# Four attention layers on one core: TensorE, not VectorE and GpSimd, sums the softmax weights of the last layer in the last two batches

## The chip, the cores and the metric

The kernel runs on one core of a Trainium2 chip. The metric is the time of one execution on the device in microseconds (us). Names of engines: PE is TensorE (PEld its weight loads), DVE is VectorE, ACT is ScalarE, POOL is GpSimd, SP is SyncE, which issues the DMAs.

## What is computed

Input x is 8 x 256 x 32 x 32 in fp32: 8 batches, 256 channels, T = 1024 tokens. Four layers follow one another, each per batch. Only the last one is changed:

```python
def _L3_conv_ref(hidden_states, ...):
    x = _group_norm(hidden_states, gn_gamma, gn_beta)
    x = x.reshape(B, C, H * W).transpose(0, 2, 1)
    q, k, v = x @ wq.T + bq, x @ wk.T + bk, x @ wv.T + bv      # 8 heads of 32 channels
    scores = jnp.einsum('bhid,bhjd->bhij', q * scale, k)        # 1024 x 1024 per head
    probs = jax.nn.softmax(scores)
    ctx = jnp.einsum('bhij,bhjd->bhid', probs, v)
    out = _layer_norm(ctx @ wo.T + bo, ln_gamma, ln_beta)
    return out + residual
```

Layers 0 to 2 (a latent attention, an attention with 32 channels of queries, an attention over all 256 channels with a group norm) are untouched. The softmax needs, for each query, the sum over 1024 keys of the weights exp(score - maximum). Who makes that sum in batches 6 and 7 of layer 3 is what changes.

## The kernel before

**Two lanes.** The program is written as five instruction streams, one per engine, with semaphores between them. Layers 0 to 2 of a batch are its front, layer 3 its back. The front of batch b + 2 runs beside the back of batch b; at the end no front is left, and the backs of batches 6 and 7 run beside each other. Batch 6 uses the tiles of lane `ba` (stacked queries `qs` and keys `ks`, values `vb`, weights `prb`, sums `accb`, banks 4 to 7 of PSUM); batch 7 uses lane `bb` (the tile `q2k` for queries and keys, `xm` for values, `pr`, `acc`, `tmp` and `xm` for weights, `w` for sums, banks 0 to 3).

**The order.** Each engine's stream for two batches is merged from two generators by a table of numbers, `ORDER[part, engine]`: so many pieces of the first, so many of the second, and so on. The part "backs" is the end of the program, with batches 6 and 7. A piece ends at a `yield`.

**A round.** The back of a batch does four heads at a time (QUAD = 4) and so has two rounds, u = 0 and 1. In a round PE first makes 32 tiles of plain scores (`max_tile`, L673, two matmuls each) of which DVE takes the maxima (`maximum`, L1358, 128 x 1024 each); the maxima go by DMA into a row of the stacked queries. Then come 16 steps (`steps`): one step is half of the queries (ic) against one of 8 tiles of keys. A step has four shifted scores (`scores` and `stacked_scores`, L687), one per head, each in one PSUM bank of 512 columns; ACT takes the exponential of each (`exps3`, L1211) into one of RING = 3 slots of weights. Every two steps (RUN = 2) PE multiplies weights and values (`weigh`, L974) for both steps: four matmuls of 32 output rows a step, in four column tiles of the array side by side, into bank 2. I call the 8 matmuls of one `weigh` a run, and the four of a step a quad. A round has 8 runs, a batch 16.

**Banks of the scores.** A score goes to `turn3[use % 3]`, that is banks 0, 1, 3 in turn, and waits until the bank's last tenant has been read (`take_turn`).

**The sums before.** DVE adds the weights of steps pair by pair into `sums` (`add_weights`, L1527, 128 x 1024: two heads at once). In batches 6 and 7 (`both_add`) DVE does the first pair of heads only, POOL the second (L607). After 8 steps PE sums the result over partitions with ones (`sum_weights`, L986, a quad) into one of the three banks, ACT makes 1 / sum from it by Ln and Exp (`invert`, L1078 and L1081), and DVE multiplies (`normalise`, L1534). ACT may reuse a slot of the ring only when the run and both adds that read it are done.

**The tail.** After both rounds come the output projection (L654), the layer norm's variance (L1014) and the rest (L1261 to L1279, L1581, L1585), and the store.

What one step costs PE now, in the kernel's words:

```python
for s in range(first, first + RUN):
    jt = s % NT
    for g in range(QUAD):
        mm = pe.matmul(o.ps[L * g:L * g + L, 2, :],
                       o.vb[:, jt, L * (QUAD * u + g):L * (QUAD * u + g + 1)],
                       weights3(o, STEPS3 * u + s, g), start=jt == 0, stop=jt == NT - 1,
                       tile_position=(0, L * g))
```

Of the kernel before, what the change touches and what calls it, by code (L numbers as in the profile page):

```python
# [29 lines left out]
ALU = mybir.AluOpType  # L30
# [7 lines left out]
CH = C // P  # L38
IC, IW = 2, 512
# [20 lines left out]
for _name, _n in (("gn_w2", 2), ("gn_b2", 2), ("bq2", 2), ("bk2", 2), ("bo2", 2), ("gn_w3", 2), ("gn_b3", 2),  # L60
# [48 lines left out]
        8, 74, 74, 51, 1, 2, 8, 1, 1, 2, 1, 2, 1, 1, 3, 1, 1, 1, 1, 1, 1, 1, 2, 1, 4, 3, 4, 1, 1, 1, 1, 2, 3,  # L109
        2, 1, 1, 5, 1, 3, 1, 17, 1, 8, 1, 3, 1, 1, 1, 5, 1, 4, 1, 2,),  # L110
# [16 lines left out]
        0, 2, 1, 12, 14, 10, 1, 1, 1, 1, 1, 1, 1, 1, 10,),  # L127
# [5 lines left out]
        6, 4, 3, 1, 4, 2, 1, 1, 2,),  # L133
# [67 lines left out]
def attention_layers(nc, x, weights, vectors, small, concepts, constants, out):  # L201
    with ExitStack() as ctx:
# [216 lines left out]
        def both_add(b):  # L419

            return b >= B - 2

        def score_use(s, g):
            return QUAD * s + g + (s >= NT + 2)
# [47 lines left out]
        def _(sp):  # L472
# [9 lines left out]
            def program(o):  # L482
# [26 lines left out]
                def back(b):  # L509
# [16 lines left out]
                    for pair in range(2):  # L526
                        sp.wait_ge(o.summed3[pair].sem, o.summed3[pair].at(b, (NT - 1) * IC * CH - 2))
# [18 lines left out]
        def _(pool):  # L546
# [7 lines left out]
            def program(o):  # L554
# [41 lines left out]
                def back(b):  # L596
                    yield "head"
                    for n in range(IC * CH if both_add(b) else 0):
                        for j in range(1, NT):
                            s = NT * n + j  # L600
                            pool.wait_ge(o.exped[3].sem, o.exped[3].at(b, QUAD * (s + 1)))
# [1037 lines left out]
```

## Time and profile before

| | |
|---|---|
| median of 3 runs | 2710.54 us (2708.7 to 2719.36) |
| the profiled execution | 2716.84 us |
| its span, first to last instruction | 2715.0 us |
| granted PE clock, mean | 0.940 of full |
| PE busy | 2536.3 us (93%) |
| DVE busy | 1870.5 us (69%) |
| ACT busy | 1281.9 us (47%) |
| POOL busy | 591.2 us (22%) |

Times of rows count from the start of the span. The stretch in which batches 6 and 7 stand alone goes from 2372 us to the end. "MATMUL x16" in a row of the trace stands for 8 matmuls of the program, since an fp32 matmul is executed as two; matmuls that read rounded operands (L673, L687) are one each. The bracket at a row's end is the idle time before it and who ended it. In the rows of stretches, the number before "(x" is busy time, and PEclk is the granted clock as a share of full speed: 0.50 is 1.2 GHz, 1.00 is 2.4 GHz.

### The profile page before, as it was taken

How to read it: one execution, taken by the hardware profiler on the slowest of the kernel's cores; microseconds unless marked ns; L12 is line 12 of the kernel's file. 1: busy time of each engine (PE TensorE's matmuls, PEld its weight loads, DVE VectorE, ACT ScalarE, POOL GpSimd, SP SyncE). 2: the span in 40 equal slices, each digit the busy share in tenths (PEclk: the TensorE clock that was granted, in tenths of full speed). 3: DMA queues.
4: the chain of work that ended last, by engine and by line, in shares of the span. 5: the costliest groups of instructions: out<-in, count | busy, mean ns of one | idle time of the engine just before them, and what ended most of it. 6: DMA issues, size and time to landing. Idle time of an engine off the chain costs nothing.

```text
span 2715.0 us, 26577 instructions
## 1 busy us (share of the span) xinstructions
PE 2536.3 (93%) x9892; PEld 1431.6 (53%) x9892; DVE 1870.5 (69%) x1925; ACT 1281.9 (47%) x2209; POOL 591.2 (22%) x322
## 2 busy tenths in 40 slices
PE   7989989999999999999999999999999999988887
PEld 4466654464654656455564646546564555544432
DVE  5544327787487865787677874878657876769995
ACT  2453221646346562555526464364625555135466
POOL 0083130050110502023010401105010130124463
PEclk8999996999999899999999999998999999978898
DMA  2000002020302003020120203010030201222201
GB/s 76 1 0 1 1 17 62 1 47 16 93 1 47 1 24 86 1 47 1 62 47 1 47 1 109 1 39 9 16 93 1 47 1 47 47 62 47 47 16 47
DMA packets 33777, 88.93 MB, mean 33 GB/s; under 512 B 10608, under 2 KB 10800, under 8 KB 33392
## 3 DMA queue, kind: packets, MB, share of 16 engines
q1 hardware_dynamic: 33648, 87.23, 12.0%
q8 instruction: 78, 1.28, 0.2%
q14 instruction: 51, 0.42, 0.1%
HBM read 19.79 MB, written 16.78 MB: 13 GB/s over the span
## 4 chain that ended last, share of the span: by engine, by line
PE 75%; DVE 15%; ACT 4%; issue 3%; POOL 2%; SPq 1%; DMA 1%; DVEq 0%; ACTq 0%; POOLq 0%
PE ps L654 11%; PE ps L687 10%; PE ps L673 9%; PE ps L805 8%; PE ps L974 7%; PE ps L896 6%; PE ps L662 6%; PE ps L809 4%; DVE ba_nmx L1358 2%; PE ps L743 2%; PE ps L882 2%; DVE fa_nmx L1358 2%; DVE accb L1527 2%; DVE bb_nmx L1358 1%; DVE w L1527 1%
## 5 line engine op out<-in xcount | busy, mean ns | idle before, releaser
L1358 DVE TENSOR_REDUCE ba_nmx<-ps 128x1 f32<-128x1024 f32 x448 | 531.3, 1219 | 115.9 <-PE ps L673 114.1
L1211 ACT ACTIVATE prb<-ps 128x512 f32<-128x512 f32 x896 | 483.9, 604 | 220.4 <-PE ps L687 215.5
L1527 DVE TENSOR_TENSOR accb<-accb,prb 128x1024 f32<-128x1024 f32 x312 | 396.1, 1303 | 78.0 <-ACT prb L1211 77.1
L687 PE MATMUL ps<-qs,ks 97*128 97x512 f32 x896 | 349.4, 479 | 20.9 <-DMA qs<-ba_nmx_r 16.3
L1069 ACT ACTIVATE pr<-ps 128x512 f32<-128x512 f32 x336 | 198.2, 604 | 334.8 <-PE ps L896 260.4
L673 PE MATMUL ps<-ks,qs 96*128 96x512 f32 x896 | 333.3, 471 | 17.7 <-DVE ba_nmx L1358 15.8
L576 POOL TENSOR_TENSOR q2k<-pr,q2k 128x512 fp32r<-128x512 f32 x112 | 147.7, 1338 | 797.5 <-ACT q2k L1106 797.5
L687 PEld LDWEIGHTS ps<-qs,ks 97*128 97x128 f32 x896 | 170.5, 203 | 215.2 <-issue 101.7
L673 PEld LDWEIGHTS ps<-ks,qs 96*128 96x128 f32 x896 | 175.3, 206 | 122.5 <-DVE ba_nmx L1358 51.4
L974 PE MATMUL ps<-prb,vb 128*32 128x512 f32 x1792 | 230.0, 633 | 0.2 <-ACT prb L1211 0.2
L1358 DVE TENSOR_REDUCE fa_nmx<-ps 128x1 f32<-128x1024 f32 x168 | 198.0, 1216 | 34.1 <-PE ps L882 18.9
L566 POOL TENSOR_TENSOR acc<-pr 128x1024 f32<-128x1024 f32 x28 | 67.4, 2407 | 689.9 <-ACT pr L1069 576.6
L805 PE MATMUL ps<-pr,h 128*128 128x512 f32 x448 | 210.7, 593 | 0.0
L809 PE MATMUL ps<-q2k 128*128 128x512 f32 x672 | 179.8, 404 | 5.3 <-ACT tmp L1097 4.1
L566 POOL TENSOR_TENSOR acc<-acc,pr 128x1024 f32<-128x1024 f32 x56 | 133.6, 2386 | 217.5 <-ACT pr L1069 217.4
L654 PE MATMUL ps<-hb,w 128*128 128x512 f32 x368 | 172.5, 613 | 2.5 <-ACT hb L1127 2.5
L896 PE MATMUL ps<-q2k 128*128 128x512 f32 x672 | 173.4, 393 | 0.0
L809 PEld LDWEIGHTS ps<-q2k 128*128 128x128 f32 x672 | 129.1, 194 | 41.1 <-POOL q2k L576 10.2
L896 PEld LDWEIGHTS ps<-q2k 128*128 128x128 f32 x672 | 126.7, 189 | 37.3 <-issue 10.3
L654 PE MATMUL ps<-h,w 128*128 128x512 f32 x272 | 128.3, 600 | 2.0 <-ACT h L1127 1.5
L805 PEld LDWEIGHTS ps<-pr,h 128*128 128x128 f32 x448 | 84.0, 189 | 64.7 <-issue 56.3
L687 PE MATMUL ps<-q2k,ks 97*128 97x512 f32 x224 | 100.1, 470 | 13.9 <-ACT pr L1069 8.4
(329 smaller groups left out, 3528.7 us busy)
## 6 DMA issues: line engine op xcount, KB each, us to landing
qs<-part SPq DMA_DIRECT2D x168, 128.0 KB, 2.5
ks<-part SPq DMA_DIRECT2D x168, 128.0 KB, 2.5
xm<-in_x SPq DMA_DIRECT2D x8, 1024.0 KB, 4.8
kept<-xm SPq DMA_DIRECT2D x8, 1024.0 KB, 4.2
prb<-kept SPq DMA_DIRECT2D x14, 512.0 KB, 3.7
out<-prb SPq DMA_DIRECT2D x28, 256.0 KB, 2.0
q2k<-part SPq DMA_DIRECT2D x48, 128.0 KB, 2.4
w<-in_weights SPq DMA_DIRECT2D x1, 2592.0 KB, 8.8
```

What stands on the lines that cost most here:

```text
L566: pool.tensor_tensor(o.acc[:], before if jg == 1 else o.acc[:], now, ALU.add).then_inc(o.summed[n].sem, 1)
L654: mm = pe.matmul(o.ps[0:m, bank, :], wcol(name, kt, m0, m), src[:, kt, cols(ic)], start=kt == 0, stop=kt == CH - 1)
L673: mm = pe.matmul(o.ps[:, bank + jc, :], queries[0:STACK, tile(it)], keys[0:STACK, cols(jc)], start=True, stop=True)
L687: return pe.matmul(o.ps[:, bank, :], keys[0:ROW + 1, tile(jt)], queries[0:ROW + 1, cols(ic)], start=True, stop=True)
L805: mm = pe.matmul(o.ps[:, 2 + ch, :], o.v[:, jt, tile(ch)], o.pr[:, t % 4, :], start=jt == 0, stop=jt == NT - 1)
L809: mm = pe.matmul(o.ps[:, 2 + ch, :], values[:, jt, tile(ch)], weights[t % 3], start=jt == 0 and weights is o.p_hi and values is o.v_hi, st ...
L896: mm = pe.matmul(o.ps[:, bank, :], kpart[:, kt, keys], qpart[:, kt, cols(ic)], start=False, stop=kt == CH - 1 and kpart is o.kl2)
L974: mm = pe.matmul(o.ps[L * g:L * g + L, 2, :], o.vb[:, jt, L * (QUAD * u + g):L * (QUAD * u + g + 1)], weights3(o, STEPS3 * u + s, g), star ...
L1069: act.activation(o.pr[:, t % 4, :], o.ps[:, bank, :], ACT.Exp).then_inc(o.exped[n].sem, 1)
L1211: act.activation(weights3(o, n, g), o.ps[:, turn3[score_use(s, g) % 3], :], ACT.Exp)\
L1358: dve.tensor_reduce(o.nmx[:, head, it:it + 1], o.ps[:, bank:bank + 2, :], AX.XY, ALU.max, negate=True).then_inc(o.max_sb[n].sem, 1)
L1527: dve.tensor_tensor(o.sums[pair], o.pairs[(now - 1) % RING][pair] if j == 1 else o.sums[pair], o.pairs[now % RING][pair], ALU.add).then_in ...
```

## The change

In batches 6 and 7 (`pe_sums`) a run of PE gets, behind the four matmuls of a step with the values, four more with ones in the place of the values, in the same column tiles, accumulated over the 8 steps into bank 3 of the lane. The adds of DVE and POOL in these batches are gone, and so are `sum_weights` and the waits on the adds. Bank 3 is no longer free for scores, so these go to banks 0 and 1 in turn, and a score waits for the exponential of the score two before. ACT takes Ln from bank 3 as soon as the run that ends 8 steps is done. The tables of the part "backs" are new for PE, ACT, DVE, POOL and SP (of PE's only the first line is shown).

```diff
     ("backs", "PE"): (
-        2, 1, 6, 1, 1, 1, 6, 1, 2, 5, 1, 2, 1, 7, 1, 4, 1, 5, 1, 3, 1, 6, 1, 2, 1, 2, 1, 6, 1, 1, 1, 8, 1, 3,
...
+        0, 1, 2, 1, 8, 1, 7, 3, 1, 2, 1, 3, 1, 4, 2, 5, 1, 7, 2, 11, 1, 2, 1, 7, 1, 1, 1, 1, 1, 8, 1, 2, 1, 4,
...
     ("backs", "DVE"): (
...
+        27, 4, 16, 1, 7, 1, 1, 6, 1, 1, 4, 22, 1, 5, 31, 1, 4, 3, 1, 2, 1, 2, 4, 2, 4,),
     ("backs", "POOL"): (
-        0, 2, 1, 12, 14, 10, 1, 1, 1, 1, 1, 1, 1, 1, 10,),
+        1,),
...
-        def both_add(b):
+        def pe_sums(b):
             return b >= B - 2

-        def score_use(s, g):
-            return QUAD * s + g + (s >= NT + 2)
+        def score_use(b, s, g):
+            return QUAD * s + g + (s >= NT + 2 and not pe_sums(b))
+
+        def score_bank(b, use):
+            return use % 2 if pe_sums(b) else turn3[use % 3]
...
                         def take_turn(use):
-                            if use >= 3:
+                            if pe_sums(b):
+                                if use >= 2:
+                                    pe.wait_ge(o.exped[3].sem, o.exped[3].at(b, QUAD * STEPS3 * u + use - 1))
+                            elif use >= 3:
                                 done, count = bank_use(o, u, use - 3)
                                 pe.wait_ge(done.sem, done.at(b, count))
-                            return turn3[use % 3]
+                            return score_bank(b, use)
...
                             if first % NT == 0 and n:
                                 pe.wait_ge(o.taken[3].sem, o.taken[3].at(b, n // NT))
+                                if pe_sums(b):
+                                    pe.wait_ge(o.logged[3].sem, o.logged[3].at(b, n // NT))
                             for s in range(first, first + RUN):
...
+                                for g in range(QUAD if pe_sums(b) else 0):
+                                    mm = pe.matmul(o.ps[L * g:L * g + L, 3, :], ones[:, 0:L],
+                                                   weights3(o, STEPS3 * u + s, g), start=jt == 0, stop=jt == NT - 1,
+                                                   tile_position=(0, L * g))
                             mm.then_inc(o.weighed[3].sem, 1)
...
-                            if s == NT + 1:
+                            if s == NT + 1 and not pe_sums(b):
                                 sum_weights(0)
                                 yield
                         weigh(STEPS3 - RUN)
                         yield
-                        sum_weights(1)
-                        yield
+                        if not pe_sums(b):
+                            sum_weights(1)
+                            yield
...
                 def invert(b, n, count, bank, into):
-                    act.wait_ge(o.total[n].sem, o.total[n].at(b, count))
+                    if n == 3 and pe_sums(b):
+                        act.wait_ge(o.weighed[3].sem, o.weighed[3].at(b, NT // RUN * count))
+                    else:
+                        act.wait_ge(o.total[n].sem, o.total[n].at(b, count))
...
-                                chunk, j = divmod(n - RING, NT)
-                                used = (NT - 1) * chunk + max(j, 1)
-                                act.wait_ge(o.summed3[pair].sem, o.summed3[pair].at(b, used))
+                                if not pe_sums(b):
+                                    chunk, j = divmod(n - RING, NT)
+                                    used = (NT - 1) * chunk + max(j, 1)
+                                    act.wait_ge(o.summed3[pair].sem, o.summed3[pair].at(b, used))
...
-                            for pair in range(1 if both_add(b) else 2):
+                            for pair in range(0 if pe_sums(b) else 2):
```

The new lines move the numbers: L673 is L662 in the changed kernel, L687 is L676, L654 is L643, L974 is L968, and the matmuls with ones are L973.

In PE's stream, first place: steps of batch 6 in its first round (`qs,ks` are its scores, `prb` its weights), with the maxima of batch 7's first round (`q2k`) between. Before:

```order
L974 MATMUL ps<-prb,vb 32x512 x8
L687 MATMUL ps<-qs,ks 128x512 x2
L673 MATMUL ps<-q2k 128x512 x2
L687 MATMUL ps<-qs,ks 128x512 x3
L673 MATMUL ps<-q2k 128x512 x2
L687 MATMUL ps<-qs,ks 128x512 x3
L974 MATMUL ps<-prb,vb 32x512 x8
```

The changed kernel, near the same place:

```order
L973 MATMUL ps<-prb,ones 32x512 x4
L676 MATMUL ps<-qs,ks 128x512 x2
L662 MATMUL ps<-q2k 128x512 x4
L676 MATMUL ps<-qs,ks 128x512 x2
L662 MATMUL ps<-q2k 128x512 x2
L676 MATMUL ps<-qs,ks 128x512 x2
L662 MATMUL ps<-q2k 128x512 x2
L968 MATMUL ps<-prb,vb 32x512 x4
L973 MATMUL ps<-prb,ones 32x512 x4
L968 MATMUL ps<-prb,vb 32x512 x4
L973 MATMUL ps<-prb,ones 32x512 x4
```

A run has gone from two quads to four, and between runs there are still 6 to 8 scores and two or more tiles of maxima.

Second place, PE's stream from the last run of batch 6 (`prb`) on, where batch 7 (`q2k`) has only itself beside it and the tail of batch 6. Before:

```order
L974 MATMUL ps<-prb,vb 32x512 x8
L986 MATMUL ps<-accb,ones 32x512 x4
L687 MATMUL ps<-q2k 128x512 x2
L654 MATMUL ps<-hb,w 128x512 x4
L687 MATMUL ps<-q2k 128x512 x3
L654 MATMUL ps<-hb,w 128x512 x4
L974 MATMUL ps<-acc,xm 32x512 x2
L974 MATMUL ps<-tmp,xm 32x512 x2
L974 MATMUL ps<-xm 32x512 x4
L687 MATMUL ps<-q2k 128x512 x3
```

The changed kernel:

```order
L676 MATMUL ps<-q2k 128x512 x4
L643 MATMUL ps<-hb,w 128x512 x4
L676 MATMUL ps<-q2k 128x512 x2
L643 MATMUL ps<-hb,w 128x512 x4
L676 MATMUL ps<-q2k 128x512 x2
L968 MATMUL ps<-acc,xm 32x512 x2
L968 MATMUL ps<-tmp,xm 32x512 x2
L973 MATMUL ps<-acc,ones 32x512 x2
L973 MATMUL ps<-tmp,ones 32x512 x2
L968 MATMUL ps<-xm 32x512 x4
L973 MATMUL ps<-xm,ones 32x512 x4
```

The sum with ones that stood behind batch 6's last run is gone, and eight scores now surround the projections, not five; five runs of batch 7 follow in either kernel.

## Rows read from the trace of the kernel before

**Rows 1.** Stretches between landmarks of the end; columns: busy time by engine, PEclk, DMA.
```profile
2413.70:2479.70 66.00, 59.13 (x255) 27.03 (x255) 58.94 (x40) 35.51 (x68) 36.87 (x14) 0.82 0.12 26
2479.70:2558.90 79.20, 69.54 (x292) 32.02 (x288) 68.38 (x57) 40.70 (x76) 37.44 (x14) 0.87 0.13 29
...
2648.70:2692.50 43.80, 39.27 (x159) 13.90 (x156) 30.08 (x15) 27.98 (x53) 25.28 (x10) 0.89 0.02 7
2692.50:2715.00 22.50, 11.73 (x28) 4.96 (x24) 9.08 (x13) 14.21 (x23) 0.00 (x0) 0.80 0.38 128
```

**Rows 2.** Waits of PE, 2413 to 2692: us in total, times, longest.
```profile
PE ps L673 <- DVE bb_nmx L1358: 11.7, 12, 2.5
PE ps L986 <- issue: 6.8, 1, 6.8
PE ps L673 <- DVE ba_nmx L1358: 6.5, 5, 2.6
PE ps L986 <- DVE w L1527: 3.6, 2, 3.2
```

**Rows 3.** Groups of DVE and POOL, 2413 to 2692: busy, mean ns, idle before.
```profile
L1358 DVE TENSOR_REDUCE bb_nmx<-ps 128x1 f32<-128x1024 f32 x57 | 66.8, 1214 | 6.8 <-PE ps L673 6.8
L1527 DVE TENSOR_TENSOR accb<-accb,prb 128x1024 f32<-128x1024 f32 x24 | 55.3, 2305 | 0.5
...
L607 POOL TENSOR_TENSOR accb<-accb,prb 128x1024 f32<-128x1024 f32 x24 | 66.4, 2768 | 28.5 <-ACT prb L1211 27.8
```

**Rows 4.** The same view of DVE from 200 to 2370, where POOL adds no such weights.
```profile
L1527 DVE TENSOR_TENSOR accb<-accb,prb 128x1024 f32<-128x1024 f32 x288 | 340.7, 1219 | 77.5 <-ACT prb L1211 77.1
```

**Rows 5.** PE in order of time: start us, us; runs, tiles of maxima, scores.
```profile
2448.89 1.92 PE L974 MATMUL ps<-prb,vb 128*32 128x512 f32 x16
...
2452.76 0.63 PE L673 MATMUL ps<-q2k 96*128 96x512 f32 x2
2453.22 1.17 PE L687 MATMUL ps<-qs,ks 97*128 97x512 f32 x3
2454.38 1.92 PE L974 MATMUL ps<-prb,vb 128*32 128x512 f32 x16
...
2616.03 1.92 PE L974 MATMUL ps<-prb,vb 128*32 128x512 f32 x16
2617.88 0.96 PE L687 MATMUL ps<-q2k 97*128 97x512 f32 x3
...
2635.21 1.06 PE L974 MATMUL ps<-xm 128*32 128x512 f32 x8
2636.09 1.04 PE L974 MATMUL ps<-pr,xm 128*32 128x512 f32 x8
```

**Rows 6.** PE and ACT in order of time; layer 0, where scores have two banks.
```profile
84.45 0.73 PE L687 MATMUL ps<-q2k,ks 97*128 97x512 f32 x2
...
84.99 1.08 ACT L1069 ACTIVATE pr<-ps 128x512 f32<-128x512 f32 x2 [3.06 <-PE ps L687]
...
86.12 0.73 PE L687 MATMUL ps<-q2k,ks 97*128 97x512 f32 x2
```

**Rows 7.** Stretches from the first to a last run of three rounds.
```profile
2419.90:2474.80 54.90, 48.27 (x213) 21.88 (x212) 50.07 (x32) 30.43 (x59) 36.70 (x14) 0.84 0.06 13
2497.40:2552.30 54.90, 49.64 (x221) 22.60 (x220) 48.74 (x35) 30.91 (x59) 33.45 (x14) 0.85 0.00 1
2571.60:2609.60 38.00, 33.11 (x149) 15.96 (x148) 37.33 (x31) 18.06 (x34) 18.21 (x8) 0.91 0.08 17
```

**Rows 8.** Two stretches of 4 us in which the granted clock fell.
```profile
2432.00:2436.00 4.00, 3.62 (x13) 1.89 (x17) 4.00 (x4) 1.57 (x3) 2.65 (x2) 0.51 0.00 0
...
2668.00:2672.00 4.00, 3.40 (x14) 1.17 (x17) 4.00 (x3) 3.71 (x8) 3.09 (x2) 0.87 0.01 2
```

**Rows 9.** PE in order of time: batch 6's last sum, batch 7's projections.
```profile
2646.80 1.94 PE L986 MATMUL ps<-accb,ones 128*32 128x512 f32 x8 [6.79 <-issue]
...
2692.49 8.30 PE L654 MATMUL ps<-h,w 128*128 128x512 f32 x16
```

More of the change, by code:

```diff
@@ L108 @@
     ("backs", "ACT"): (
-        8, 74, 74, 51, 1, 2, 8, 1, 1, 2, 1, 2, 1, 1, 3, 1, 1, 1, 1, 1, 1, 1, 2, 1, 4, 3, 4, 1, 1, 1, 1, 2, 3,
-        2, 1, 1, 5, 1, 3, 1, 17, 1, 8, 1, 3, 1, 1, 1, 5, 1, 4, 1, 2,),
+        8, 74, 74, 49, 1, 1, 2, 2, 1, 1, 3, 1, 1, 2, 3, 1, 1, 1, 1, 2, 2, 1, 1, 2, 4, 1, 1, 1, 3, 2, 2, 1, 2,
+        2, 5, 1, 1, 1, 10, 1, 1, 3, 8, 1, 4, 1, 2, 1, 14, 1, 3, 1, 4, 1, 2,),
     ("fronts", "DVE"): (
@@ L132 @@
     ("backs", "SP"): (
-        6, 4, 3, 1, 4, 2, 1, 1, 2,),
+        6, 4, 3, 1, 4, 1, 1, 1, 1, 1, 1,),
 }
@@ L525, in back @@
                     sp.wait_ge(o.weighed[3].sem, o.weighed[3].at(b, CH * STEPS3 // RUN - 1))
-                    for pair in range(2):
+                    for pair in range(0 if pe_sums(b) else 2):
                         sp.wait_ge(o.summed3[pair].sem, o.summed3[pair].at(b, (NT - 1) * IC * CH - 2))
@@ L597, in back @@
                     yield "head"
[L598 to L601, printed above, removed]
-                            if j == 1 and n:
-                                pool.wait_ge(o.total[3].sem, o.total[3].at(b, n))
-                            done = o.summed3[1]
-                            if j > 1:
-                                pool.wait_ge(done.sem, done.at(b, (NT - 1) * n + j - 1))
-                            pool.tensor_tensor(o.sums[1], o.pairs[(s - 1) % RING][1] if j == 1 else o.sums[1],
-                                               o.pairs[s % RING][1], ALU.add).then_inc(done.sem, 1)
-                            yield
                 return front, back
@@ L960, in scores @@
                             for g in (2 * pair, 2 * pair + 1):
-                                bank = take_turn(score_use(s, g))
+                                bank = take_turn(score_use(b, s, g))
                                 stacked_scores(bank, o.queries[:, g, :], o.keys[:, g, :], jt, ic).then_inc(o.scored[3].sem, 1)
@@ L1204, in exps3 @@
                                 act.wait_ge(o.weighed[3].sem, o.weighed[3].at(b, (n - RING) // RUN + 1))
-                                chunk, j = divmod(n - RING, NT)
-                                used = (NT - 1) * chunk + max(j, 1)
-                                act.wait_ge(o.summed3[pair].sem, o.summed3[pair].at(b, used))
+                                if not pe_sums(b):
+                                    chunk, j = divmod(n - RING, NT)
+                                    used = (NT - 1) * chunk + max(j, 1)
+                                    act.wait_ge(o.summed3[pair].sem, o.summed3[pair].at(b, used))
                             if n == g == 0 and o.before(b) is not None:
                                 act.wait_ge(o.stored.sem, o.stored.at(o.before(b), 16 * 4))
-                            act.activation(weights3(o, n, g), o.ps[:, turn3[score_use(s, g) % 3], :], ACT.Exp)\
+                            act.activation(weights3(o, n, g), o.ps[:, score_bank(b, score_use(b, s, g)), :], ACT.Exp)\
                                 .then_inc(o.exped[3].sem, 1)
@@ L1241, in steps @@
                         for s in range(STEPS3):
-                            if s == NT + 2:
-                                yield from invert(b, 3, IC * u + 1, turn3[total_use(0) % 3], o.rdenb[:])
+                            if s == (NT + 1 if pe_sums(b) else NT + 2):
+                                yield from invert(b, 3, IC * u + 1, 3 if pe_sums(b) else turn3[total_use(0) % 3], o.rdenb[:])
                             yield from exps3(u, s, 0)
@@ L1250, in steps @@
                         yield
-                        yield from invert(b, 3, IC * u + 2, turn3[total_use(1) % 3], o.rdenb[:])
+                        yield from invert(b, 3, IC * u + 2, 3 if pe_sums(b) else turn3[total_use(1) % 3], o.rdenb[:])
                     def nothing(u):
@@ L1568, in steps @@
                                 yield from normalise(u, 0)
-                            for pair in range(1 if both_add(b) else 2):
+                            for pair in range(0 if pe_sums(b) else 2):
                                 if s % NT:
```

1 line of the change is left out of this document (removed), and 13 rows, old and new, of the table ORDER.

## The prediction, written before the changed kernel ran

> **What bounds the kernel now.** The whole page says PE 93% busy, but the change touches only the end, so I read the stretches between landmarks first, from the first shifted score of batch 6 at 2413.7 us to the end [rows 1]. They take 301 us. Call them B (steps of batch 6 beside maxima of batch 7), C (the reverse), D (second steps of 6 beside second maxima of 7), E (steps of both), F (steps of 7 alone, with the tail of 6) and G (the tail of 7). In B and C the busy columns of PE and DVE are alike, near 90% each, and the granted clock is 0.82 and 0.87: part of PE's busy time is work at 1.2 GHz. PE's waits name the cause [rows 2]: 18.2 us for a DVE maximum, the rest for a sum that DVE or POOL had not finished. DVE is late because its own adds are slow: 2305 ns here [rows 3] against 1219 ns for the same instruction where POOL adds nothing [rows 4]; POOL's own take 2768 ns. Behind such a wait PE's clock falls, as at 2432, where 4 us had 0.51 of the full clock [rows 8]. So the end is bound by DVE with POOL at its side, and PE pays twice, by the wait and by the clock.
>
> **What the change removes.** DVE loses 56 adds of a pair of heads (28 per batch, 7 per sum), 24 of them the accb row at 2305 ns: some 120 us of DVE, and POOL loses its whole part, 56 at about 2.75 us. DVE keeps the maxima, 1214 ns each [rows 3], three per run at most in B and C, so it is idle half the time, and none of PE's waits in rows 2 has a reason any more. PE loses 8 sums with ones, 1 us each.
>
> **What it adds to PE.** A run of two quads occupies PE for 1.85 us (2616.03 to the next start at 2617.88) and a further quad for 0.88 us (2635.21 to 2636.09) [rows 5]. Four quads are 1.85 + 2 x 0.88 = 3.6 us. There are 32 runs, so 56 us more, less 8 us of sums: 48 us of PE at full clock, none of it beside other PE work. Against it stand the waits of PE that the change can end, 11.7 + 6.8 + 6.5 + 3.6, 29 us [rows 2], and the work done at half clock: by the clocks of B, C and F, 0.82, 0.87 and 0.89 [rows 1], it averaged about 0.86, that is 28% of 279 us at 1.2 GHz, some 78 us, which at 2.4 GHz would have been 39. 29 + 39 - 48 = 20 us of gain, if PE could always be fed. I don't think that it can.
>
> **The two banks.** With two banks, a score can be issued only when the exponential two before has ended. Where layer 0 works with two banks [rows 6], the exponentials start 0.54 us after the scores (84.45 to 84.99), two of them take 1.08, so the second starts 0.48 after the first and one lasts 0.60, and the next scores follow 0.05 later (86.07 to 86.12). A pair of exponentials thus costs at least 0.60 + 0.05 + 0.54 = 1.19 us without anything between. During a run PE has at most two scores lying ready, so ACT does two exponentials and then idles; the other six of the two steps must follow in 3 pairs. From one run's start to the next: run 3.6, first score to exponential 0.54, two full pairs 2 x 1.19, the last pair 0.48 + 0.60, and 0.3 for the last score before the run: 7.9 us. A tile of maxima is 0.46 us to the next start, at 2452.76 [rows 5], and some 0.1 more where scores wait; such tiles partly fit the 0.7 us that PE has free in each pair, so I take 8.1 in B and C with about two tiles a run, and 8.8 in D, where the order has about six.
>
> Now the stretches of runs before [rows 7]. B: seven intervals in 54.9 us, 7.84 each; after 7 x 8.1 = 56.7, **+1.8**. C: the same 54.9, **+1.8**. D: four intervals in 38.0 us, 9.5 each; after 35.2, **-2.8**. Before and after these intervals the longer last run (+1.75) and the sums and waits gone (about -1.1 and -0.7) cancel: 0.
>
> E, counted from D's last run (its start is about 2609.6) to the first score behind batch 6's last sum (2648.7): 39.1 us before, of which 6.8 are the wait for POOL's sum and 1.9 the sum at half clock [rows 9]. After: seven runs, four of batch 6 from 2609.6 on and three of batch 7, so 7 x 3.6 = 25.2, and 49 scores in five groups; four banks over two batches let ACT run at 0.48 an exponential, of which four are hidden by each run. I come to 17 us for the groups, 42 in all: **+3**.
>
> F: 43.8 us before [rows 1]. After: 9 us for eight scores round two blocks of projections (four matmuls each, some 3.5 us, a little under half of the 8.30 for eight [rows 9]), five runs at 3.6 = 18, then stretches of 5.0 and 5.2 (with the variance of batch 6, two matmuls of about 0.9 in the gaps) and two of 4.3: 45.8, **+2**.
>
> G: 22.5 us [rows 1], starting with the projections of 8.30 us, in part at half clock [rows 9]. Ln now follows the last run at once, but half of the projections (4 us) hides Ln, Exp and the multiplication anyway, so only the clock can give: **-0.7**.
>
> Sum at full clock: 1.8 + 1.8 - 2.8 + 3 + 2 - 0.7 = +5. Then the clock. At 2668 it fell to 0.87 although PE showed 3.40 us of work in 4 [rows 8], in exactly F's pattern of single scores behind exponentials with gaps of 0.2 to 0.4 us. In the changed kernel this pattern is the rule. I charge one fall more in F than before: a run at half clock is 3.6 us longer; with it **+8 us**. The Trainium skill, page "TensorE: Matmul & The Clock Gate", section "A second HAM failure mode: psum-queue depth-cycling", says that cycling through PSUM banks with micro-idles between groups makes the clock oscillate; by that rule every run of B, C and F would be at risk, not one.
>
> Another rule would raise the price of a quad. "TensorE: Matmul & The Clock Gate", "Measured speedup vs the span model", gives three column tiles of 512 columns a speedup of 2.38, not 3. By it an estimate for a quad would be some 25% above a perfect one, about 0.2 us more, and 56 quads more would add 11 us to the sum; the row of 0.88 us is of this kernel's own quads, about one fourth of four projection matmuls, and decides.
>
> Against the profiled execution's 2716.84 us the sum is 2725; that execution lies 6.3 us above the median of the runs, so I forecast 2719 us, 0.3% above 2710.54. A measurement of this kernel tells about 0.5% (13.6 us) from no change.
>
> **The bounds.** The period of 7.9 us holds only if PE stands in the chain as I say. If maxima fill the gaps completely and scores are never late, the least is PE's own work: a run, eight scores at 0.23 (three take 0.96 us [rows 5], two 0.73 [rows 6]), two tiles and 0.3 for the switches: 3.6 + 1.9 + 1.1 + 0.3 = 6.9 us; then B and C give 8 us more each, D 3, E 5: -24 against my sum, 2695. The other bound is a period of 8.6 with a fall of clock at every third run: below, 2750.
>
> **Rivals.** (1) *PE fed after all, faster* (chance 0.23). Place: B and C, where the best interval of runs was 5.5 us with three banks (2448.89 to 2454.38 [rows 5]). For it: DVE and POOL were what PE waited for [rows 2], and the clock below 0.87 [rows 1] came from these waits; with the adds gone it returns. Against it: two banks do not allow a period under 7.9. It decides from a mean period in B and C of 7.2 us on. Time: 2719 - 24 = 2695. (2) *The clock* (chance 0.34, slower). Between runs PE has 8 scores of 0.23 us and two tiles of 0.46, 2.8 us of work in 4.4 us; in F 1.9. If every third of the 21 intervals of B, C and F falls, the run behind it takes 7.2, not 3.6 us, and the scores about 0.5 us more: 7 x 4.1 = 29 us, less the one fall that I have: 2719 + 25 = 2744. It decides from four falls on. For it: rows 8; against it: the first of these rows stands behind a wait of over 2 us, and the change takes such waits away. (3) *The adds were hidden and the sums' waits are all* (0.05): E and G give back 6.8 + 3.2 us, and the rest stays as before, 2703; PE's waits for DVE [rows 2] speak against it. My own case, the two effects nearly in balance, has 0.38.
>
> **Numbers.** My case spans 2706 to 2730. The range reaches to the middle of (1) and past that of (2): 2694 to 2750, leaving out 2 in 10. Faster by over 0.5% is under 2697: most of (1), nothing else: 0.23. Slower is over 2724: nearly all of (2) and the upper end of my case: 0.37. The rest, 0.40, is within.
>
> **What would show it.** The adds gone from DVE and POOL; starts of runs (L968, first of `vb`) 3.6 us before the next score, and 7.9 to 8.3 apart in B and C at full clock; ACT idle 2 to 3 us in each period, ended by PE's scores; PE's longest waits short and for ACT, none over 1 us for DVE before E's end; clock over 0.95 in B to E. I am wrong if the periods are under 7.2 us, if the clock in B to F is no better than the 0.86 of before, or if a run of four quads takes clearly more than 3.6 us at full clock.

## The result and the profile after

Before 2711.86 us (median of 4 runs), after 2752.24 us (2749.29 to 2753.53): the change makes the kernel 1.43% slower, ratio 1.0143, 95% interval 1.0121 to 1.0166. I had forecast 2719 us and a range to 2750; the result lies 2 us beyond it. The profiled execution took 2753.53 us, its span is 2751.7 us, 36.7 more than before.

The stretches of the end of the changed kernel, in the order B, C, D, E, F, G (columns as in [rows 1]):

```profile
2416.30:2494.20 77.90, 72.96 (x366) 29.76 (x366) 26.04 (x23) 37.73 (x69) 0.00 (x0) 0.87 0.06 13
2494.20:2582.70 88.50, 81.10 (x401) 34.59 (x400) 44.40 (x44) 40.41 (x73) 0.00 (x0) 0.92 0.15 35
2582.70:2641.00 58.30, 53.58 (x274) 25.41 (x270) 38.97 (x36) 28.73 (x52) 0.00 (x0) 0.94 0.19 42
2641.00:2682.90 41.90, 39.38 (x236) 13.91 (x236) 0.00 (x0) 22.82 (x45) 0.00 (x0) 0.92 0.07 26
2682.90:2730.40 47.50, 43.34 (x227) 15.82 (x223) 4.09 (x6) 31.16 (x57) 0.00 (x0) 1.00 0.10 33
2730.40:2751.70 21.30, 10.55 (x28) 4.46 (x24) 9.08 (x13) 13.87 (x22) 0.00 (x0) 0.85 0.19 74
```

Against [rows 1], B is 11.9 us longer and C 9.3. D and E together are 10.4 longer, F 3.7, G 1.2 shorter, and B begins 2.6 us later. The DVE column fell as forecast (59 to 26 us in B) and POOL's is 0. PE's columns rose, and the clock of B and C is 0.87 and 0.92: it came back only in part, and of B to E none reaches the 0.95 that I had named as a sign. In F it is 1.00.

PE's waits from 2413 to 2692, the same view and stretch as [rows 2]:

```profile
PE ps L676 <- ACT prb L1214: 5.3, 16, 0.7
PE ps L662 <- DVE bb_nmx L1361: 3.0, 6, 1.4
PE ps L676 <- DVE part L1356: 2.4, 1, 2.4
```

The waits for a sum are gone, and those for DVE's maxima fell from 18 us to 4. One of these is still 1.4 us, and one for another result of DVE 2.4, where I had expected none over 1 us. New are the many short waits for an exponential: 34 with those of batch 7's tiles, 10.7 us in all, none over 0.7. One interval of runs in B, in PE's order of time (start, duration; the bracket is the idle time before the row):

```profile
2442.64 0.99 PE L676 MATMUL ps<-qs,ks 97*128 97x512 f32 x2 [0.41 <-ACT prb L1214]
2443.83 0.99 PE L676 MATMUL ps<-qs,ks 97*128 97x512 f32 x2 [0.19 <-ACT prb L1214]
2444.75 1.92 PE L968 MATMUL ps<-prb,vb 128*32 128x512 f32 x8
2446.43 1.94 PE L973 MATMUL ps<-prb,ones 128*32 128x512 f32 x8
2448.14 1.09 PE L968 MATMUL ps<-prb,vb 128*32 128x512 f32 x8
2449.05 1.04 PE L973 MATMUL ps<-prb,ones 128*32 128x512 f32 x8
2450.02 0.74 PE L676 MATMUL ps<-qs,ks 97*128 97x512 f32 x2
2451.20 0.99 PE L676 MATMUL ps<-qs,ks 97*128 97x512 f32 x2 [0.45 <-ACT prb L1214]
...
2473.31 1.06 PE L968 MATMUL ps<-prb,vb 128*32 128x512 f32 x8
2474.19 1.04 PE L973 MATMUL ps<-prb,ones 128*32 128x512 f32 x8
...
2476.88 0.73 PE L676 MATMUL ps<-qs,ks 97*128 97x512 f32 x2
```

At full clock a run is 3.57 us (2473.31 to 2476.88). The run at 2444.75 takes 5.27: its first two quads are at half clock, though PE's waits since the run before it (2435.05) were 0.41 and 0.19 us. Not every fall is of this kind. The half clock of 2417 to 2427 and that of 2510 to 2519 stand behind the long waits that head B and C:

```profile
2416.33 0.47 PE L676 MATMUL ps<-qs,ks 97*128 97x512 f32 x1 [1.61 <-issue]
2509.93 1.19 PE L676 MATMUL ps<-q2k 97*128 97x512 f32 x2 [2.43 <-DVE part L1356]
```

And ACT, in its own order of time, idles behind every run, waiting for scores:

```profile
2469.15 4.87 ACT L1214 ACTIVATE prb<-ps 128x512 f32<-128x512 f32 x8 [3.54 <-PE ps L676]
2477.41 4.65 ACT L1214 ACTIVATE prb<-ps 128x512 f32<-128x512 f32 x8 [3.40 <-PE ps L676]
```

### The profile page after: what moved, and what is told of

Read it like the earlier page. It is cut to its first block, busy times and chain, and to the rows that moved or that the text cites. A ratio compares the mean times of both kernels' runs of the same rounds, so it can differ in the third digit from the quotient of the medians.

```text
span 2751.7 us, 27244 instructions
## 1 busy us (share of the span) xinstructions
PE 2588.1 (94%) x10340; PEld 1445.4 (53%) x10340; DVE 1747.3 (63%) x1869; ACT 1288.3 (47%) x2209; POOL 437.5 (16%) x266
## 4 chain that ended last, share of the span: by engine, by line
PE 79%; DVE 11%; ACT 5%; issue 3%; POOL 1%; SPq 1%; DMA 1%; DVEq 0%; ACTq 0%; POOLq 0%
PE ps L676 12%; PE ps L643 11%; PE ps L662 9%; PE ps L794 8%; PE ps L968 8%; PE ps L885 6%; PE ps L651 6%; PE ps L798 5%; PE ps L732 2%; PE ps L871 2%; DVE fa_nmx L1361 2%; PE ps L973 2%; DVE ba_nmx L1361 2%; PE ps L772 1%; PE ps L882 1%
## 5 line engine op out<-in xcount | busy, mean ns | idle before, releaser
L1530 DVE TENSOR_TENSOR accb<-accb,prb 128x1024 f32<-128x1024 f32 x288 | 340.6, 1218 | 77.8 <-ACT prb L1214 77.4
L676 PE MATMUL ps<-qs,ks 97*128 97x512 f32 x896 | 356.2, 482 | 26.2 <-DMA qs<-ba_nmx_r 16.3
L662 PE MATMUL ps<-ks,qs 96*128 96x512 f32 x896 | 331.9, 471 | 12.5 <-DVE ba_nmx L1361 11.1
L676 PEld LDWEIGHTS ps<-qs,ks 97*128 97x128 f32 x896 | 169.8, 202 | 228.6 <-ACT prb L1214 108.2
L662 PEld LDWEIGHTS ps<-ks,qs 96*128 96x128 f32 x896 | 176.3, 206 | 113.0 <-DVE ba_nmx L1361 45.1
L968 PE MATMUL ps<-prb,vb 128*32 128x512 f32 x1792 | 232.1, 631 | 0.3 <-ACT prb L1214 0.3
L643 PE MATMUL ps<-hb,w 128*128 128x512 f32 x368 | 172.8, 615 | 5.2 <-DVE ba_nmx L1361 2.7
L643 PE MATMUL ps<-h,w 128*128 128x512 f32 x272 | 128.0, 597 | 2.4 <-ACT h L1129 1.5
L1361 DVE TENSOR_REDUCE bb_nmx<-ps 128x1 f32<-128x1024 f32 x64 | 75.4, 1219 | 67.0 <-PE ps L662 66.9
```

What stands on the lines that cost most here:

```text
L643: mm = pe.matmul(o.ps[0:m, bank, :], wcol(name, kt, m0, m), src[:, kt, cols(ic)], start=kt == 0, stop=kt == CH - 1)
L662: mm = pe.matmul(o.ps[:, bank + jc, :], queries[0:STACK, tile(it)], keys[0:STACK, cols(jc)], start=True, stop=True)
L676: return pe.matmul(o.ps[:, bank, :], keys[0:ROW + 1, tile(jt)], queries[0:ROW + 1, cols(ic)], start=True, stop=True)
L968: mm = pe.matmul(o.ps[L * g:L * g + L, 2, :], o.vb[:, jt, L * (QUAD * u + g):L * (QUAD * u + g + 1)], weights3(o, STEPS3 * u + s, g), star ...
L1361: dve.tensor_reduce(o.nmx[:, head, it:it + 1], o.ps[:, bank:bank + 2, :], AX.XY, ALU.max, negate=True).then_inc(o.max_sb[n].sem, 1)
L1530: dve.tensor_tensor(o.sums[pair], o.pairs[(now - 1) % RING][pair] if j == 1 else o.sums[pair], o.pairs[now % RING][pair], ALU.add).then_in ...
```

## The experiments

Medians; each ratio is against runs of the kernel before on the same chip (2712 to 2715 us). "The end" is the stretch from 2372 us to the last instruction, "lost to the clock" is its length times what the clock lacks of 1 (an upper bound, since a slow clock costs nothing where PE waits), and a fall is a stretch of 4 us, from 2412 to G, with a granted clock under 0.90. There are 25 falls before and 19 after. Rows, falls and losses are those of the one profiled execution of each kernel, which can lie some us off its median.

### What the adds were worth, and what the ones cost

**No adds.** The kernel before in its own order, without the adds of DVE and POOL in batches 6 and 7; `sum_weights` sums a fixed tile in their place, so the softmax sums are left out:

```diff
-                                if s % NT:
-                                    add_weights(u, s, pair)
-                                    yield
+                                if s % NT:
+                                    if not both_add(b):
+                                        add_weights(u, s, pair)
+                                    yield
```

> The kernel before, its own order and three banks, with the adds of DVE and POOL in batches 6 and 7 left out and a constant summed in their place (output not the reference's). It measures what the adds cost: PE's waits of 29 us and half of some 78 us at half clock give 40 to 60 us, so 2650 to 2670, if DVE's slowness was the bound as I read it; if it comes out over 2695, the adds were worth little and the change had little to gain from the start. Against the run with three banks and few ones it gives the new order alone: within 10 us of each other if the order matters little.

Measured 2665.21 us, ratio 0.9827 (0.9807 to 0.9848): the adds cost 48 us, more than the 29 us of waits in [rows 2]. The clock accounts for the rest: what the end loses to it falls from 51 us (343.0 us at 0.85) to 27 (296.7 at 0.91), and five of the seven intervals of runs in B are 5.5 us.

**All ones, three banks, old order.** As above, with the ones in each run; they go to bank 2, so scores keep three banks. The quads with the values multiply ones too (the values are left out):

```diff
-                                                   o.vb[:, jt, L * (QUAD * u + g):L * (QUAD * u + g + 1)],
+                                                   ones[:, 0:L] if pe_sums(b) else
+                                                   o.vb[:, jt, L * (QUAD * u + g):L * (QUAD * u + g + 1)],
...
+                                for g in range(QUAD if pe_sums(b) else 0):
+                                    mm = pe.matmul(o.ps[L * g:L * g + L, 2, :], ones[:, 0:L],
```

> The kernel before with its own order and its three banks for scores; no adds on DVE and POOL in batches 6 and 7; PE has all the matmuls with ones in its runs, accumulated into bank 2 upon the values' (so the context is not told apart from the sums, and the output is not the reference's). Against the same with the new order (2721 us) it gives the price of the order alone at full ones. Theory (the parts add up: 2665 without adds and ones, and 37 us for seven eighths of the ones with three banks): 2702 to 2707. Rival (the new order costs nothing once the ones fill PE, it only seemed to cost 19 us where PE had room): 2718 to 2724, as with the new order. Second rival (the old order was made for short runs and suits long ones badly): over 2726.

Measured 2716.49 us, ratio 1.0014 (1.0005 to 1.0023). The ones cost 51 us against the run without adds, as much as the adds had cost. The end, of this run and of the one without adds:

```profile
2372.00:2712.60 340.60, 308.86 (x1604) 139.33 (x1604) 145.08 (x156) 174.55 (x328) 0.00 (x0) 0.94 0.17 44
```
```profile
2372.00:2668.70 296.70, 266.40 (x1156) 124.48 (x1156) 145.45 (x156) 175.31 (x328) 0.00 (x0) 0.91 0.19 50
```

PE has 42 us more, the end is 44 us longer. My 2702 from adding the parts was 14 us low, and the rival's 2718 nearer: the 37 us that seven eighths of the ones cost in the new order (below) was too little for this one.

**All ones, three banks, new order.** The changed kernel with that edit and `score_bank` back to `turn3[use % 3]`.

> The changed kernel with three banks for scores again (0, 1, 3); the matmuls with ones go into bank 2, that of the values, so that PE has every matmul it had. Left out: the values (ones stand in their place in batches 6 and 7), so the output is not the reference's. Theory A, two banks: with a third score lying ready, ACT has 0.6 us more to do in each run, the 28 intervals between runs fall from 8.4 to 9 us to below 8, and the time from 2752 to about 2730. Theory B, PE's own work: runs of 3.6 us and scores fill PE, a bank more changes nothing, 2745 or more. Theory C, the clock: as B, unless the granted clock of 2416 to 2494 us rises over its 0.87.

Measured 2721.22 us, ratio 1.0035 (1.0023 to 1.0047). So with all the ones the new order costs 5 us against the old one. The third bank is worth 31 us against the change.

**Few ones.** The changed kernel, ones only in the last of each 8 steps (the sums leave out seven eighths), with two banks and with three:

```diff
-                                for g in range(QUAD if pe_sums(b) else 0):
+                                for g in range(QUAD if pe_sums(b) and jt == NT - 1 else 0):
```

> The changed kernel with ones only in the last of eight steps (7 of 8 quads with ones left out, so the sums and the output are not the reference's); still two banks. Theory B: 56 quads at 0.88 us are 49 us of PE, all of it on the path: 2703. Theory A: run and chain of exponentials stand behind one another, so the run's 1.5 us come off each of 28 intervals too, 43 us, but the clock, with more short gaps per time, gives some back: 2715 to 2725. If the time stays over 2735, neither holds.

> Both: three banks and one quad with ones in eight steps, no adds anywhere (values left out as in the run with three banks, sums incomplete). It is what the end costs when the sums are nearly free, in the new order. Theory A: the difference to two banks with few ones is again 15 to 20 us, near 2695. Theory B: under 5 us of difference.

Two banks: 2708.86 us, ratio 0.9985 (0.9974 to 0.9996). Three: 2683.76 us, ratio 0.9892 (0.9875 to 0.991). The bank costs 25 us here; 56 quads cost 43 us with two banks and 37 with three, 0.77 and 0.67 us each, under the 0.88 that one lasts: a part is given back. These runs don't tell how much of that is time that PE had free and how much a better clock (0.89 to 0.90, and 0.91 to 0.95). With few ones the new order costs 19 us against the old one, with all of them 5.

**The bank alone.** The kernel with three banks and the new order, its scores in banks 0 and 1; bank 3 stays empty.

```diff
-            return turn3[use % 3]
+            return use % 2 if pe_sums(b) else turn3[use % 3]
...
-                                if use >= 3:
-                                    pe.wait_ge(o.exped[3].sem, o.exped[3].at(b, QUAD * STEPS3 * u + use - 2))
+                                if use >= 2:
+                                    pe.wait_ge(o.exped[3].sem, o.exped[3].at(b, QUAD * STEPS3 * u + use - 1))
```

> The kernel with three banks (2721 us) word for word, but its scores use banks 0 and 1 only; all quads multiply ones and accumulate into bank 2, bank 3 stays empty (the values are left out, the output is not the reference's). Against the 2721 us it is the price of the third bank alone. Theory (where the sums go does not matter): 2752 +- 3. Rival (bank 3's own traffic, its Ln and its waits for the copy, were part of the 31 us): 2735 to 2745.

Measured 2753.64 us, ratio 1.015 (1.0137 to 1.0164): 32 us for this edit, and where the sums are kept does not matter.

### Why the third bank is worth so much

**Runs cut in two.** The whole change; the second step of each run comes two scores later.

```diff
-                            for s in range(first, first + RUN):
+                            for s in range(first, first + RUN) if part is None else (first + part,):
...
+                                if behind is not None and g == 2 * pair + 1:
+                                    weigh(behind, 1)
```

> The whole change, but each run of PE is cut in two: the step 2r goes where the run stood, the step 2r + 1 behind the next two scores, so that PE is away from the scores for 1.8 us twice, not for 3.6 us once. Theory (the two-bank chain plus the ones that lie in it; ACT idles 3.4 to 3.5 us behind each run): ACT gets two exponentials between the halves, the interval of runs in B and C falls from 9.1 and 8.6 us by the 0.7 us that my chain of waits gives, the idle time of ACT in front of an exponential from 3.4 to about 1.8 us, and the time falls by 15 to 25 us from 2752 to about 2732. Rival (PE is simply full, 73 of 78 us in B, and its clock sets the time): cutting moves nothing, 2750 +- 5. Second rival (the slots of the ring come free later, since the second half ends later): slower than 2752, up to 2765.

Measured 2755.74 us, ratio 1.0158 (1.0145 to 1.0171): no gain where I had expected 15 to 25 us. ACT's idle time was cut up (1.7 and 2.4 us in place of 3.5), the intervals of undisturbed runs stayed at 7.7 to 8.6 us, and 21 falls remained. So ACT's idle time behind a long run was not what set the time.

**Half exponentials.** Each exponential covers 256 of 512 columns and PE reads them twice, which leaves out half of the weights; 383 ns of ACT instead of 597. With two banks, and with three (values left out).

```diff
-                            act.activation(weights3(o, n, g), o.ps[:, score_bank(b, score_use(b, s, g)), :], ACT.Exp)\
+                            part = slice(0, 256 if pe_sums(b) else 512)
+                            act.activation(weights3(o, n, g)[:, part], o.ps[:, score_bank(b, score_use(b, s, g)), part], ACT.Exp)\
```

> The whole change, two banks, but each shifted exponential of batches 6 and 7 covers only 256 of 512 columns, and PE reads these twice in its place (output not the reference's); an exponential takes some 0.3 us instead of 0.54, a pair in the chain of two banks about 0.5 us less. Theory (the third bank's 31 us are waits for exponentials and the clock that falls behind them): the time falls by 15 to 31 us, to 2721 to 2737, and the granted clock of the end rises. Rival (the bank's price is not the wait for ACT, but the alternation of two banks on PE itself, or PE's order): 2752 less 5 at most.

> The same halved exponentials with three banks for the scores and the ones in bank 2 (values left out of the check of sums, output not the reference's). It is the measure for the run with two banks. Theory (with three banks PE hardly waits for ACT): 2721, less 6 at most. Rival (ACT counts here too): 2700 to 2710.

Two banks: 2729.41 us, ratio 1.0051 (1.0038 to 1.0063), 23 us less. Three: 2707.19 us, ratio 0.9973 (0.996 to 0.9985), 14 less, where I had expected at most 6: ACT counts with three banks too. Falls: 19 to 11, and 5 to 3. Lost to the clock: 38 us (379.7 at 0.90) to 28 (354.6 at 0.92) with two banks, 17 (343.9 at 0.95) to 17 (330.3 at 0.95) with three, so that less than half of the 23 us and nearly none of the 14 are clock. 22 us remain between two and three banks.

**Filled gaps.** Two banks, sums in bank 2, and more work for PE: 92 scores into the empty bank 3 that nobody reads.

```diff
+                            if pe_sums(b) and s and not (pair and s % RUN == 0):
+                                stacked_scores(3, o.queries[:, 2 * pair, :], o.keys[:, 2 * pair, :], jt, ic)
```

> As the two banks with sums in bank 2, and PE issues one more score of 512 columns into the empty bank 3, read by nobody, ahead of every pair of scores except those right behind a run: 92 of them, 0.23 us each, 21 us of PE, where PE otherwise waits 0.2 to 0.5 us for ACT. Theory (the clock falls behind these waits, and its falls are most of the bank's price): half of the added work lies in waits, 10 us are on the path, the falls of the clock in B, C and E go from 12 or so windows of 4 us to under 6, which returns 10 to 18 us; 2740 to 2752. Rival (the clock does not care for gaps of this size, the waits themselves are the price): the falls stay, and the time goes up by 8 to 21 us, 2760 to 2773.

Measured 2746.96 us, ratio 1.0135 (1.012 to 1.0149): 92 matmuls more, and the median is 6.7 us less than that of the same kernel without them. The two sets of runs overlap (2743.66 to 2753.40 and 2749.55 to 2756.63), so a gain is not shown. What the runs show is that 21 us of added work cost no time that they can tell. The end with three banks, with two, and with two and the gaps filled:

```profile
2372.00:2715.90 343.90, 308.31 (x1598) 136.28 (x1598) 140.61 (x145) 175.67 (x328) 0.00 (x0) 0.95 0.16 42
```
```profile
2372.00:2754.80 382.80, 339.42 (x1604) 142.31 (x1604) 146.90 (x158) 182.75 (x328) 0.00 (x0) 0.89 0.15 39
```
```profile
2372.00:2741.80 369.80, 336.01 (x1693) 154.08 (x1692) 143.01 (x151) 183.01 (x328) 0.00 (x0) 0.94 0.16 41
```

Lost to the clock are 17, 42 and 22 us (to 2 us, the clock has two digits); the falls are 5, 18 and 7. The same three stretches of B, with two banks and then with the gaps filled:

```profile
2428.00:2432.00 4.00, 3.33 (x13) 1.47 (x9) 1.01 (x1) 2.94 (x6) 0.00 (x0) 1.00 0.00 0
2432.00:2436.00 4.00, 4.00 (x18) 1.03 (x22) 0.22 (x1) 1.51 (x3) 0.00 (x0) 0.57 0.00 0
2440.00:2444.00 4.00, 3.40 (x13) 1.14 (x16) 1.59 (x2) 3.20 (x6) 0.00 (x0) 0.84 0.02 4
```
```profile
2428.00:2432.00 4.00, 3.79 (x29) 1.26 (x31) 0.82 (x1) 2.17 (x4) 0.00 (x0) 1.00 0.00 0
2432.00:2436.00 4.00, 3.79 (x22) 1.94 (x14) 1.56 (x2) 1.72 (x4) 0.00 (x0) 1.00 0.00 0
2440.00:2444.00 4.00, 3.77 (x27) 1.47 (x16) 0.00 (x0) 1.67 (x4) 0.00 (x0) 1.00 0.00 0
```

Before the fall at 2432 PE issued pairs of scores with waits of 0.45 and 0.22 us between (3.33 us busy of 4); with these filled (3.79) the fall is gone. Six of the seven falls that are left stand behind the waits that filling didn't touch, of 1.6 us (the head of B) and 3.1 us (the head of C).

So most of the bank's price is clock. Its 32 us are a difference of medians; the two profiled executions lie 39 us apart, and 42 - 17 = 25 of these are loss to the clock, while 14 are not. Filling returns 20 of the 25. Its 92 x 0.23 = 21 us of PE cost some 7 us, since these two executions lie 13 us apart; the rest lay in waits. These are the fastest execution of the one kernel and the slowest of the other, though: of the four runs with filled gaps, that of 2753.40 us had a mean clock of 0.944 over the whole program, no better than the 0.942 to 0.945 without. The "micro-idles" of "TensorE: Matmul & The Clock Gate" in the Trainium skill (the section on depth-cycling that the prediction cites) are these, and in B the trace agrees with that rule. In F of the changed kernel it doesn't: waits of the same size stand there at a clock of 1.00, such as these.

```profile
2706.80 0.98 PE L676 MATMUL ps<-q2k 97*128 97x512 f32 x2 [0.49 <-ACT xm L1214]
2707.99 0.99 PE L676 MATMUL ps<-q2k 97*128 97x512 f32 x2 [0.20 <-ACT pr L1214]
```

Short waits can bring a fall, then, and need not; no run here tells what decides.

### Other places for the adds

Since adds and ones cost the same, I looked for a cheaper way to add. First, who adds, in the kernel before:

```diff
+        def pool_adds(b, u):
+            return both_add(b) and not (b == B - 1 and u)
...
+                                    if both_add(b) and not pool_adds(b, u):
+                                        add_weights(u, s, 1)
```

**DVE adds all** (`return False`).

> The kernel before, but DVE does POOL's adds of batches 6 and 7 as well, each behind its own of the same step; POOL adds nothing. Theory (POOL's company makes DVE's adds slow: 2.31 us beside it, 1.22 alone, so two alone cost DVE no more than one beside POOL): the accb group of DVE doubles in number with a mean of 1.2 to 1.3 us, DVE's busy time stays within 15 us, and the time stays within 5 us of 2713, with up to 7 us less where PE waited for POOL's last sum. Rival (the slow adds are not POOL's doing, but the ring's and the banks'): DVE's adds stay at 2.3 us, DVE gets 130 us more work, and the time goes over 2760.

**DVE adds all in the last round** (as in the diff).

> The kernel before, but in the second round of batch 7 alone (E and F), where DVE has few maxima or none, DVE does POOL's 14 adds. Theory: an add costs 1.22 us there instead of 2.75 on POOL, both pairs are ready some 0.3 us earlier in each step, and the last sum does not wait for POOL: 2 to 6 us less than 2713. Rival (PE and ACT set the pace of F, the adds are hidden on either engine): 2713 +- 2. Against: DVE gets late for the normalisation and the variance of batch 6, slower by 3 us or more.

**POOL adds in C and D only** (`return both_add(b) and b + u == B - 1`).

> The kernel before, with POOL adding only in the second round of batch 6 and the first of batch 7 (C and D); in B, and in E and F, DVE does both pairs. The runs with DVE alone had shown B 4 us shorter and D 3.5 us longer than with POOL, and E and F shorter. Theory (the places add up): 4 us less than with DVE in the last round only, 2695 to 2697. Rival (B's gain is lost again in C, where both wait for the same maxima): 2699 to 2702.

Measured 2704.66, 2699.53 and 2699.51 us, ratios 0.9969 (0.9957 to 0.998), 0.9957 (0.9941 to 0.9973) and 0.9938 (0.9924 to 0.9952). With DVE alone, its adds:

```profile
L1533 DVE TENSOR_TENSOR accb<-accb,prb 128x1024 f32<-128x1024 f32 x48 | 56.0, 1215 | 0.0
```

Twice the adds of [rows 3] in the same 56 us: it was POOL's company that made one cost 2305 ns. DVE in the last round gains 14 us by the medians and 12 by the ratio, of which I had expected 2 to 6. The profiled executions lie 22 us apart: 10 before D's last run, where the edit changes nothing, and 12 behind it, where PE's 6.8 us of waiting for POOL's sum is gone and PE waits once for DVE:

```profile
PE ps L992 <- DVE accb L1533: 2.9, 1, 2.9
```

POOL in C and D only gives no more in the median; the intervals of the two overlap.

**The last step summed directly.** PE sums the last step's weights itself, a quad more per sum; 6 adds are left, not 7.

```diff
+                            for g in range(QUAD if both_add(b) else 0):
+                                pe.matmul(o.ps[L * g:L * g + L, bank, :], ones[:, 0:L], weights3(o, NT * (n + 1) - 1, g),
+                                          start=True, stop=False, tile_position=(0, L * g))
                             for done in o.summed3:
-                                pe.wait_ge(done.sem, done.at(b, (NT - 1) * (n + 1)))
+                                pe.wait_ge(done.sem, done.at(b, adds(b) * (n + 1)))
```

With POOL in C and D; with POOL everywhere but in the last round; with POOL in all rounds:

> As the run with POOL in C and D only, and besides PE takes the last of the 8 steps of each sum straight from the weights: a quad with ones on the last step's weights, then the quad on the added ones, in the same bank. DVE and POOL add 6 times a sum, not 7: 8 adds of DVE (2.3 us) fewer, up to 8 of POOL, and PE gets 8 quads of 0.88 us, 7 us. Theory (in B to D DVE is what PE waits for, a quad costs what it lasts): 16 to 20 us of DVE gone against 7 of PE; about 5 us less than without this, 2690. Rival (PE is what counts now, as with all the ones): 5 to 7 us more. Second rival (the slot of the last step is held till the sum, ACT waits): 10 us more.

> PE takes the last step of each sum straight from the weights, 6 adds a sum are left; POOL adds everywhere except in the second round of batch 7. Theory: the two gains add as before, 6 us less than 2699.5: 2693. Rival (with fewer adds the place of POOL matters more, B has 4 adds and 3 maxima an interval on DVE alone): 2688 to 2691. Second rival: B is better with DVE alone, 2695 to 2698.

> The kernel before with the direct sum of the last step alone, POOL adds in all four rounds. The last sums of E and F then wait for 6 adds of POOL, not 7, and PE's longest wait for a sum (6.8 us) should go. Theory: 7 us of PE against 20 us of DVE and POOL: 2703 to 2708 beside 2713. Rival (the gain comes only with DVE at the end): 2712 to 2720.

Measured 2693.07, 2694.49 and 2700.7 us, ratios 0.9923 (0.9911 to 0.9936), 0.9937 (0.9925 to 0.9949) and 0.9962 (0.9949 to 0.9975). Alone it gives 11 us (I had expected 5 to 10), on top of the other change 5 to 6, since both end the same wait: the 6.8 us are gone in the run with it alone too. In the first of the three PE's largest waits behind 2590 us are short (total, times, longest):

```profile
PE ps L682 <- DVE bb_nmx L1374: 1.0, 2, 0.6
PE ps L696 <- DMA q2k<-bb_nmx_r: 0.9, 1, 0.9
```

It is the fastest kernel with all of the computation, if not clearly ahead of the second: 0.8% faster than before, 2.2% than the change.

## Why the prediction was wrong

The parts in one chain, each step one edit (the runs are of three chips, on which the kernel before takes 2712 to 2713 us):

| | us | step |
|---|---|---|
| before | 2713 | |
| no adds | 2665 | -48 |
| all ones, three banks, old order | 2716 | +51 |
| new order | 2721 | +5 |
| two banks | 2754 | +32 |
| the change | 2752 | |

The idea is even: 51 us of PE for 48 us of waits and clock. The loss is the bank that the sums take from the scores.

The profiled execution is 36.7 us longer than before, where the sum said 8. By stretch, the change forecast and measured:

| | forecast | measured |
|---|---|---|
| intervals of B and C | +3.6 | +13.9 |
| D | -2.8 | +1.6 |
| E | +3 | +8.8 |
| F, with the fall charged | +5 | +3.7 |
| G | -0.7 | -1.2 |
| the edges | 0 | +9.9 |

By the steps of the prediction:

- **A run of four quads, 3.6 us: right**, 3.57 measured. The 48 us that the ones add to PE (net of the old sums) fit too: PE is busy 47 us more in the end (336.3 for 288.9), in part by luck, since the clocks differ (0.90 for 0.85); the old order with all the ones is busy 42 us more than without adds.
- **The adds go and the waits of rows 2 with them: right** but for 4 us of waits for maxima. I put 29 us of waits and up to 39 of clock on that side; the run without adds gives 48 of these 68.
- **The interval of 8.1 us in B and C: nearly right at full clock, and in part by luck.** The intervals of B at full clock are 8.05 to 8.47 us. In the seven of B (63.7 us, clock 0.91) 5.7 us are lost to the clock, which leaves 8.3 each; in C (60.0 us, 0.98) 1.2, which leaves 8.4. But the chain that I derived it from asked for 0.7 us less with cut runs, and they kept 7.7 to 8.6.
- **The clock: the step that failed.** "I charge one fall more in F than before", 3 us on the sum. That sum set the new intervals at full clock against old ones that held their falls, so it took for granted that B and C would lose all of theirs. They lost a part: 25 falls became 19, and in F, where I had put the new fall, the clock was 1.00. In the place of the 3 us the trace has some 15: 7 in the intervals of B and C, 3.3 in E (0.93), and 5 more than before at the edges. From the edit itself: one bank less loses 25 us to the clock. This is rival 2, to which I gave 0.34 and 2744 us, and in B the rule on depth-cycling that I cited for it; I held against it that a fall wants a wait of over 2 us before it, from one row of [rows 8], though the other row there, at 2668 with gaps of 0.2 to 0.4 us, was already of the kind that came. Three of B's falls, at 2432, 2444 and 2460, come behind waits of at most 0.66 us; its first comes behind 1.61.
- **The edges: set to 0 without a reason that held, +9.9 measured.** B starts 2.6 us late, and 3.1 and 4.2 us come around the intervals of B and C, with falls at 2416 to 2428 and 2508 to 2520. About half of it is the clock counted above.
- **D, -2.8 forecast, +1.6 measured.** Its four intervals are 9.9 us, not 8.8, at clock 1.00 with PE busy 37.7 of 39.6 us: with about six tiles an interval PE is full, and the tiles do not hide in the gaps as I assumed.
- **E and F.** E took 47.9 us from D's last run to 2682.9, not 42; what is not clock are groups of scores that cost more than my 17 us. F took 47.5, not 45.8, at clock 1.00.

So of 29 us of error the clock is about 12, the largest term and less than half: the rest is D (4), the edges at full clock (5), the intervals of B and C (3), E (2.5) and F (2).

What stays open: the 14 us of the bank's price between the two profiled executions that are not clock, why the same short waits bring a fall in B and none in F, and why the new order costs 19 us with few ones and 5 with all. The bank's price in the old order was not measured.

## What to carry to other kernels

A buffer taken from the stage that feeds the busiest engine can cost more than the work that it saves: price it with the clock, as the falls times the work behind each, and look in the trace for falls that stand behind short waits alone, as well as behind long ones. Where an old interval holds falls of the clock, compare it with the new one at the same footing, both with their falls or both without. And two engines that add side by side may be no faster than one: look up the same instruction where the other engine is idle, before buying a third helper.

## What the runs showed that I had not expected

- In B of the changed kernel, from 2432 us on, the clock fell three times behind waits of 0.19 to 0.66 us, none longer; 21 us of useless scores in such waits cost no time, and took the falls of the profiled execution from 18 to 7.
- DVE's add of 128 x 1024 takes 1215 ns alone and 2305 ns beside POOL's own of 2768 ns: together they add two tiles in 2.8 us, DVE alone in 2.4.
- An exponential of 256 columns takes 383 ns, one of 512 takes 597: 0.84 ns a column and some 0.17 us fixed.
